# First expert layer's end summed by diagonal products, router indices reordered, and a written order for the causal attention's head groups

## The chip, the cores and the metric

The kernel runs on one NeuronCore of a Trainium2 chip. The metric is the time of one execution on the device in microseconds (us); the statement about the kernel before is the median of three runs. The program is written by hand for each engine: TensorE (PE; its weight loads are PEld), VectorE (DVE), ScalarE (ACT), GpSimd (POOL) and SyncE (SP), with semaphores between them. Each engine carries out its own list in order, so a wait holds up everything behind it on that engine.

## The reference, cut to what matters

There are 1,024 tokens of width 512. The six layers are: bottleneck layer, sigmoid attention, bottleneck layer, experts, causal attention, experts. Each begins with a layer norm.

```python
# experts (layers 4 and 6): H, F, E, K = 512, 800, 8, 2
logits = xt @ gate_w.T
top_vals, top_idx = top_k(softmax(logits), K)          # two of eight experts for each token
act = silu(x @ w1[e].T) * (x @ w3[e].T)
y   = sum over a token's two experts of weight * (act @ w2[e].T)
x   = x + 0.5 * y
# causal attention (layer 5): 32 heads of 16
q, k, v = x @ wq.T, x @ wk.T, x @ wv.T                 # q and k are rotated (rotary)
out = softmax(causal(q @ k.T / 4)) @ v
x   = x + out @ wo.T
```

## The kernel before, in words

The tokens lie in eight tiles of 128 rows (`X`, f32, in SBUF). A layer's front normalizes each tile on DVE (`bn_stats`, `bn_aggr`, then the subtraction and scaling), with POOL working out the reciprocal deviation between the last two; PE transposes the result and ACT copies it out of PSUM. `dve_front` (L463) interleaves the tiles: in turn n it does the update of tile n, the statistics of n-1, the normalization of n-2 (in layers 5 and 6) and the moments of n-1.

**Experts.** `dve_moe` sorts the 2,048 (token, expert) pairs into 72 blocks of 32 rows, which form four streams of 18 steps. The router is a chain of small DVE operations (L1131 to L1184): one-hot matrices OHL (L1160) and OHH (L1162 to L1165), a product of 16 small matmuls on PE that inverts the permutation (L1011), then the indices GIDX for the gather (L1178 to L1180). Between the two lie the experts of the blocks (EBC to EBX, L1168 to L1174) for which SP waits before it issues the step's weight loads (L921, L874), and FALL (L1175), for which ACT waits. PE fills its waits with throw-away bf16 products (`pe_awake`, L996): 14 while the router works and 18 while the first rows are gathered. A weight load whose expert has not changed, or was guessed right, is skipped by its condition.

A step is 128 rows: `up` (L1033), SiLU on ACT (L1093), product and block transposes on DVE (L1205, L1221), `down` (L1052) and the last 32 inner columns (L1066). ACT copies the result (L1105) and POOL scatters it to DRAM (L979). At the layer's end SP and ACT wait for the last scatter (`y_out`), and each issues eight loads of rows (`rows_back`, L960), SP those of a token's first expert and ACT those of its second. DVE adds the two, weighted, with two operations on each tile (L1226, L1227), in `dve_front`'s turn.

**Between experts and attention.** `sp_attn1_weights` (L1358) waits for the last product (`m_y`), then issues three loads of 1,024 KB: the q and k weights into WRAW and the v weights into WQKV. After its row loads, ACT reorders q and k in 16 copies (L1372). PE waits for the first updated tile, does ten throw-away products and then the fronts of tiles 0 to 3 with three such products between them (`pe_front_attn1`, L1446), and then projections (L1432).

**Causal attention.** Eight groups of four heads. All engines follow one list, `PLAN1`, made by `plan_attn1` (L1249). Its units in a group are: 32 `max` (PE scores for the row maxima, L1480; DVE takes the maximum, L1638), `shift` (DVE, L1643 to L1647) and `mtr` (PE transposes L1487, DVE copy L1655, SP sends the result, L1406); 48 `exp` (PE scores L1504, and the mask L1507 on a diagonal tile; ACT exponential L1585); 12 `av` (PE products with the values, L1517); 2 `oc` (ACT copy L1592) and 2 `turn` (PE transposes L1526; DVE L1663, L1664). The maxima run ahead of the exponentials: each unit of group g has a due time, from a count of the columns before it, with `LEAD1 = 1.25` groups taken off for the maxima, and the list is sorted by it. `max`, `mtr` and `turn` share four PSUM banks in a ring (`lay_ring`): a `max` of over 512 columns, an `mtr` and a `turn` take two neighbouring banks, other maxima one. PE waits before each of them until DVE has done with what was in the banks. The `exp` units have three banks, `av` one.

## Time and profile before

| | us |
|---|---|
| median of 3 runs (1286.12 to 1288.74) | 1287.13 |
| the profiled execution | 1285.68 |
| its span in the trace | 1283.8 |
| PE busy in the span | 1176.7 (92%) |
| DVE busy | 869.8 (68%) |
| ACT busy | 356.2 (28%) |
| POOL busy | 141.0 (11%) |

In the timelines each row is: start, duration, engine, line, operation, output<-input, count, and in brackets how long the engine sat idle before it and what ended that. The time from one row's start to the next is called its pitch below; it is shorter than the duration where operations overlap in the pipeline. The stages lie as follows in the span: first router about 183 to 201, first expert layer to 503, front and projections of attention to 635, head groups to 889, output product and second router to 953, second expert layer to the end.

### The profile page before, as it was taken

The page shows a single profiled execution, that of the slowest core. Times are in us where ns is not written, and L with a number is a line of the kernel's source. Part 1 is how long each engine was busy: PE and PEld are TensorE (multiplying, and loading weights), DVE is VectorE, ACT ScalarE, POOL GpSimd, SP SyncE. Part 2 cuts the span into 40 slices and gives each one's busy share as a digit, 9 for nine tenths or more (in the row PEclk, how much of TensorE's full clock was granted, in tenths as well). Part 3 has the DMA queues.
Part 4 walks back from the last instruction along what each step waited for, and adds up shares of the span by engine and source line. Part 5 has one row for each costly group of instructions (what it writes and reads, how often), then busy time and mean ns, then how long its engine had stood idle before and what let it go on. Part 6 is the DMA issues. An engine that isn't in the chain of part 4 may idle for free.

```text
span 1283.8 us, 28073 instructions
## 1 busy us (share of the span) xinstructions
PE 1176.7 (92%) x9925; PEld 507.6 (40%) x9925; DVE 869.8 (68%) x2481; ACT 356.2 (28%) x744; POOL 141.0 (11%) x191
## 2 busy tenths in 40 slices
PE   7799979999999995799999999998989899999992
PEld 3478553333333331343333333333644233333330
DVE  4832666877777762778888888850458677777763
ACT  5434611000000000322266666665200000000010
POOL 2200011111111100442000000000110101111000
PEclk9899969999999998899999999999979999999996
DMA  9100342258714354429514332003951645615556
GB/s 361 43 1 1 152 159 101 62 193 297 253 53 153 100 174 150 151 76 191 129 27 83 51 47 31 2 2 123 390 193 35 255 141 202 202 52 186 183 186 239
DMA packets 63667, 174.31 MB, mean 136 GB/s; under 512 B 9885, under 2 KB 16627, under 8 KB 61351
## 3 DMA queue, kind: packets, MB, share of 16 engines
q1 hardware_dynamic: 54319, 148.50, 35.9%
q0 software_dynamic: 5760, 18.88, 4.4%
q10 hardware_dynamic: 3448, 5.14, 1.2%
q8 instruction: 78, 1.28, 0.4%
q14 instruction: 62, 0.51, 0.1%
HBM read 785.47 MB, written 22.03 MB: 629 GB/s over the span
## 4 chain that ended last, share of the span: by engine, by line
PE 77%; DVE 11%; DMA 5%; ACT 3%; issue 3%; SPq 2%; POOL 0%; ACTq 0%; POOLq 0%; DVEq 0%
PE PS L1033 29%; PE PS L1052 13%; PE PS L1517 6%; PE PS L1480 5%; PE PS L1504 4%; PE PS L760 3%; PE PS L744 2%; PE PS L1544 2%; PE PS L1432 2%; PE PS L524 2%; DVE PS L1638 2%; PE PS L1066 1%; PE PS L508 1%; DVE STAT L472 1%; DMA split_scratch<-arena 1%
## 5 line engine op out<-in xcount | busy, mean ns | idle before, releaser
L1033 PE MATMUL PS<-arena 128*32 128x400 f32 x3456 | 394.4, 499 | 7.9 <-DMA HH<-in_w 3.9
L1033 PE MATMUL PS<-HH,arena 128*32 128x400 f32 x1152 | 393.8, 500 | 0.0
L1033 PEld LDWEIGHTS PS<-arena 128*32 128x32 f32 x3456 | 143.4, 110 | 252.4 <-issue 244.3
L1221 DVE STREAM_TRANSPOSE arena<-arena 32x192 f32<-32x192 f32 x576 | 211.3, 367 | 7.2
L1638 DVE CUSTOM_DVE_ANT_0 PS<-PS,U 128x128 f32<-128x128 f32 (+7 forms) x256 | 187.8, 785 | 35.4 <-PE PS L1480 34.4
L1052 PE MATMUL PS<-arena 128*32 128x512 f32 x1512 | 193.8, 596 | 4.0 <-DVE arena L1221 4.0
L1585 ACT ACTIVATE arena<-PS 128x512 f32<-128x512 f32 (+3 forms) x384 | 165.1, 497 | 74.5 <-PE PS L1507 49.0
L1199 DVE STREAM_TRANSPOSE arena<-arena 32x128 f32<-32x128 f32 x544 | 164.5, 302 | 17.9 <-DMA arena<-h_scratch,RT 9.9
L1093 ACT ACTIVATE arena<-PS 128x400 f32<-128x400 f32 x72 | 36.2, 503 | 432.3 <-PE PS L1033 432.3
L1205 DVE TENSOR_TENSOR arena<-arena,PS 128x400 f32<-128x400 f32 x72 | 41.0, 571 | 131.9 <-ACT arena L1093 131.9
L1033 PEld LDWEIGHTS PS<-HH,arena 128*32 128x32 f32 x1152 | 124.7, 110 | 0.0
L1504 PE MATMUL PS<-arena 99*128 99x512 bf16 (+3 forms) x384 | 111.2, 328 | 3.9 <-ACT arena L1585 2.2
L1480 PE MATMUL PS<-arena 96*128 96x512 bf16 (+3 forms) x384 | 101.0, 328 | 11.0 <-DVE arena L1638 6.2
L1052 PEld LDWEIGHTS PS<-arena 128*32 128x32 f32 x1512 | 56.2, 111 | 127.5 <-issue 121.7
L1052 PE MATMUL PS<-HH,arena 128*32 128x512 f32 x216 | 100.3, 601 | 0.0
L1517 PE MATMUL PS<-arena 128*32 128x512 f32 (+3 forms) x768 | 80.2, 497 | 0.0
L969 POOL DMA_INDIRECT arena<-h_scratch,RT x36 | 35.2, 978 | 356.1 <-DVE arena L1199 309.6
L490 POOL TENSOR_SCALAR VE<-MV 128x1 f32<-128x1 f32 (+1 forms) x44 | 12.8, 290 | 489.3 <-DVE MV L480 416.0
L1480 PEld LDWEIGHTS PS<-arena 96*128 96x128 bf16 x384 | 30.6, 97 | 80.0 <-DVE arena L1638 51.6
L979 POOL DMA_INDIRECT y_scratch<-arena,RT x36 | 35.5, 986 | 236.5 <-ACT arena L1105 231.6
L1432 PE MATMUL PS<-HH,arena 128*128 128x512 f32 x128 | 57.9, 613 | 1.6 <-ACT HH L532 0.9
L1504 PEld LDWEIGHTS PS<-arena 99*128 99x128 bf16 x384 | 36.9, 97 | 54.5 <-ACT arena L1585 35.0
(247 smaller groups left out, 1239.2 us busy)
## 6 DMA issues: line engine op xcount, KB each, us to landing
arena<-in_w SPq DMA_DIRECT2D x456, 800.0 KB
arena<-in_w2a SPq DMA_DIRECT2D x266, 768.0 KB
HH<-in_w SPq DMA_DIRECT2D x152, 800.0 KB
HH<-in_w2a SPq DMA_DIRECT2D x38, 768.0 KB
arena<-split_scratch SPq DMA_DIRECT2D x96, 128.0 KB, 6.8
split_scratch<-arena SPq DMA_DIRECT2D x8, 768.0 KB, 5.6
arena<-in_w2b SPq DMA_DIRECT2D x72, 64.0 KB
U<-in_w2b SPq DMA_DIRECT2D x72, 64.0 KB
```

The source lines that it names most:

```text
L760: mm = eng.matmul(PS[:, bank, jj * P:(jj + 1) * P], AT0[:, m % 4, j * P - a:(j + 1) * P - a], h_in[:, i, h * P:(h + 1) * P], start=(i == 0 ...
L1033: mm = eng.matmul(PS[SR * j:SR * j + SR, 2 * hf + m, 0:FH], XBT[:, u, c, SR * j:SR * j + SR], W13[j][:, c // 2, m, c % 2, hf * FH:(hf + 1) ...
L1052: mm = eng.matmul(PS[SR * j:SR * j + SR, 4 + u, :], ACT_T[:, u, c, SR * j:SR * j + SR], half_of(j, half)[:, c % (FC // 2), :], start=(c == ...
L1199: tr = eng.transpose(XBT[SR * b:SR * b + SR, u, :, SR * a:SR * a + SR], src[:, :, SR * b:SR * b + SR])
L1205: eng.tensor_tensor(half, half, PS[:, 2 * hf + 1, 0:FH], ALU.mult).then_inc(S("m_act"), 1)
L1221: tr = eng.transpose(ACT_T[SR * b:SR * b + SR, u, :, rows], src[:, :, SR * b:SR * b + SR])
L1432: mm = eng.matmul(PS[:, at + par, :], WQKV[:, x, c, first:first + P], HS[k][1][:, c, J * HT_:(J + 1) * HT_], start=(c == 0), stop=(c == C ...
L1480: mm = eng.matmul(PS[:, b + lo // HT_, 0:hi - lo], QT[0:KS, slot, h, i * P:(i + 1) * P], KT[0:KS, slot, h, lo:hi], start=True, stop=True)
L1504: mm = eng.matmul(bank[:, 0:hi - lo], KT[0:KS + 3, slot, h, i * P:(i + 1) * P], QT[0:KS + 3, slot, h, lo:hi], start=True, stop=not diag, s ...
L1517: mm = eng.matmul(PS[32 * h:32 * h + 32, 7, lo - J * HT_:HT_], VA[:, i, (GH * g + h) * VC:(GH * g + h) * VC + 32], PB[:, n % 3, h, 0:hi - lo],
L1585: eng.activation(PB[:, (n // GH) % 3, h, 0:hi - lo], PS[:, 4 + n % 3, 0:hi - lo], ACT.Exp, scale=SCALE1).then_inc(S("s_p"), 1)
L1638: eng.tensor_tensor_reduce(scores, scores, MASKW[:, T - wide:T], 1.0, HOLE, ALU.add, ALU.max, MP[:, g % 2, h, i:i + 1]).then_inc(S("s_md"), 1)
```

## The change

Four things change together.

**The first expert layer's end.** WRAW moves to where the weights of stream 1 lie. The k weights are loaded on SP as soon as the last `up` is done (before the last step's `down` weights); those of q and v follow behind the last step's loads, with no wait for `m_y`. SP issues all 16 row loads, tile by tile; ACT none, and it reorders the weights as soon as its last copy is done, k first. DVE makes eight matrices (`DIAG`, 128x128, identity times a column of weights) after its last transposes. For tiles 0 to 3 (`SUMMED`) PE adds the two weighted rows, as two f32 products with `DIAG` in a bank (`pe_sum_rows`), and DVE adds the bank to X in one operation. PE does 34 throw-away products after its last `down`, then the four sums, then the fronts with two such products between them. The DVE order of the front is written out in `dve_front_attn1`.

**The router.** The eight operations on constants (L1120 to L1127) move ahead of the last two `dve_top` of the first expert layer. OHH's third part is made ahead of OHL, its second part by ACT (`s_rowed`), and PE waits for both `s_low` and `s_rowed`. FOUND, FROM and GIDX come ahead of EBC to EBX and FALL.

**The front of the sixth layer.** The last tile's `bn_aggr` comes ahead of the normalization of tile 6.

**The attention's list.** The due times give way to a written order of 98 units for every group (`GROUP1`): m is the next of the maxima, `shift` and `mtr`, e an `exp`, a an `av`, c an `oc`, t a `turn`. A group's order begins with the last `av`, `oc` and `turn` of the group before as its first a, c, t. Ahead of it run the 34 units of group 0 and ten of group 1.

```diff
-        WRAW = arena[:, 26464:26464 + 2 * C * D].rearrange("p (n c d) -> p n c d", n=2, c=C)
+        at = 7584 + 2 * (2 * C * FF + FC * D)
+        WRAW = arena[:, at:at + 2 * C * D].rearrange("p (n c d) -> p n c d", n=2, c=C)
+        DIAG = arena[:, at + 2 * C * D:at + 2 * C * D + 8 * P].rearrange("p (n d) -> p n d", d=P)
+        SUMMED = (0, 1, 2, 3)
...
+        def dve_front_attn1(eng, k, update):
...
+            for n in range(4):
+                update(n)
+                if n >= 1:
+                    stats(n - 1)
+                if n >= 2:
+                    normal(n - 2)
+                if n >= 1:
+                    moments(n - 1)
+            stats(3)
+            normal(2)
+            moments(3)
+            for n in range(4, NT):
+                update(n)
+                if n == 4:
+                    normal(3)
+                stats(n)
+                if n > 4:
+                    normal(n - 1)
+                moments(n)
+            normal(NT - 1)
...
+                if p == NSTEP and f == 0:
+                    eng.wait_ge(S("m_h"), 2 * NSTEP)
+                    eng.dma_start(WRAW[:, 1], A["wqkv"][:, 1]).then_inc(S("s_wraw1"), 16)
...
             for i in range(NT):
                 rows_back(eng, i, 0)
+                if f == 0:
+                    rows_back(eng, i, 1)
...
             if f == 0:
                 eng.drain().then_inc(stage_end, 1)
+                pe_awake(eng, 0, 34)
+                eng.wait_ge(S("s_diag"), 1)
                 pe_front_attn1(eng, k + 1)
...
+        def pe_sum_rows(eng, k, i):
+            eng.wait_ge(yl_in[i], 16 * TOPK)
+            if i >= 2:
+                eng.wait_ge(s_x, NT * (k + 1) + i - 1)
+            for j in range(TOPK):
+                mm = eng.matmul(PS[:, 6 + i % 2, :], DIAG[:, TOPK * i + j, :], YT[:, i, j, :], start=(j == 0), stop=(j == TOPK - 1))
+            mm.then_inc(S("s_sum"), 1)
...
         def act_moe(eng, link, k, f):
+            eng.wait_ge(S("s_high"), f + 1)
+            eng.activation(OHH[:, :, 1, :], OHH[:, :, 2, :], ACT.Copy, scale=row_of[:]).then_inc(S("s_rowed"), 1)
...
+            if f == 0:
+                eng.wait_ge(S("m_h"), 2 * NSTEP)
+                for i in SUMMED:
+                    for j in range(TOPK):
+                        dg = eng.tensor_scalar(DIAG[:, TOPK * i + j, :], ident[:], WT[:, i, j:j + 1], None, ALU.mult)
+                dg.then_inc(S("s_diag"), 1)
+
             def add_rows(i):
+                if f == 0 and i in SUMMED:
+                    eng.wait_ge(S("s_sum"), i + 1)
+                    eng.tensor_tensor(X[:, i, :], X[:, i, :], PS[:, 6 + i % 2, :], ALU.add).then_inc(s_x, 1)
+                    return
...
-        LEAD1 = 1.25
+        GROUP1 = ("emememeacmeetemeaemememeaemeemeaemeemeacemeteemam"
+                  "meemmemeameemeemmaeeeeammmeeemmemamemeeeamememeea")
...
+                next_of = dict(zip("meact", (later, iter(exps), iter(sums), iter(copies), iter(turns))))
+                for kind in GROUP1:
+                    u = next(next_of[kind], None)
+                    if u is not None:
+                        plan.append(u)
...
         def sp_attn1_weights(eng):
-            eng.wait_ge(S("m_y"), NSTEP)
-            for n in (1, 0):
-                eng.dma_start(WRAW[:, n], A["wqkv"][:, n]).then_inc(S("s_wraw"), 16)
+            eng.dma_start(WRAW[:, 0], A["wqkv"][:, 0]).then_inc(S("s_wraw0"), 16)
             eng.dma_start(WQKV[:, 2], A["wqkv"][:, 2]).then_inc(S("s_wv"), 16)
...
         def pe_front_attn1(eng, k):
-            eng.wait_ge(s_x, NT * k + 1)
-            pe_awake(eng, 0, 10)
+            for i in SUMMED:
+                pe_sum_rows(eng, k - 1, i)
             for i in range(4):
                 pe_front(eng, k, i)
                 if i < 3:
-                    pe_awake(eng, 0, 3)
+                    pe_awake(eng, 0, 2)
```

## Rows read from the trace of the kernel before

**Rows 1.** The page, part 4: the chain that ended last, by engine.

```profile
PE 77%; DVE 11%; DMA 5%; ACT 3%; issue 3%; SPq 2%; POOL 0%; ACTq 0%; POOLq 0%; DVEq 0%
```

**Rows 2.** POOL, SP, DVE and PE timelines at the first expert layer's end.

```profile
503.28 0.97 POOL L979 DMA_INDIRECT y_scratch<-arena,RT  x1 [7.35 <-ACT arena L1105]
...
502.42 0.84 SPq L1362 DMA_DIRECT2D arena<-in_wqkv  x2
...
510.75 4.35 SPq L960 DMA_DIRECT2D arena<-y_scratch  x8
...
514.47 0.75 DVE L1226 SCALAR_TENSOR_TENSOR X<-arena,RT,X 128x512 f32<-128x512 f32 x1 [18.52 <-DMA arena<-y_scratch]
...
531.34 9.43 PE L1432 MATMUL PS<-HH,arena 128*128 128x512 f32 x16 [0.88 <-ACT HH L532]
```

**Rows 3.** Busy time by stretch: engines, PE clock, DMA share, GB/s, first layer's end.

```profile
506.00:508.00 2.00, 0.00 (x0) 0.00 (x0) 0.00 (x0) 0.00 (x0) 0.00 (x0) 0.50 1.00 385
```

**Rows 4.** POOL and DVE timelines at the second expert layer's end.

```profile
1261.40 0.97 POOL L979 DMA_INDIRECT y_scratch<-arena,RT  x1 [9.05 <-ACT arena L1105]
...
1267.70 0.75 DVE L1226 SCALAR_TENSOR_TENSOR X<-arena,RT,X 128x512 f32<-128x512 f32 x1 [15.33 <-DMA arena<-y_scratch]
```

**Rows 5.** Chain of waits (start, us, what) and DVE timeline: a projection, a PSUM addition.

```profile
541.64 6.87 PE PS L1432 x16
...
920.64 0.69 DVE L1669 TENSOR_TENSOR X<-X,PS 128x512 f32<-128x512 f32 x1 [2.99 <-PE PS L1544]
```

**Rows 6.** DVE, PE and SP timelines, first router; last row the second router's PE.

```profile
183.45 0.06 DVE L1120 MEMSET RT<- 128x4 uint32 x1 [0.24 <-DVEq L158]
...
184.69 0.29 DVE L1131 TENSOR_TENSOR RT<-small,RT 128x128 f32<-128x128 f32 x1
...
194.62 0.21 DVE L1178 COPY RT<-PS 128x54 f32<-128x54 f32 x1
...
193.49 0.57 PE L1011 MATMUL PS<-arena 128*128 128x54 bf16 x16 [1.85 <-DVE arena L1165]
193.91 5.73 PE L996 MATMUL PS<-identb 128*128 128x512 bf16 x18
199.79 0.66 PE L1017 MATMUL PS<-ident,arena 128*128 128x128 f32 x4
...
199.12 0.13 SPq L874 DMA_DIRECT2D HH<-in_w  x1
...
951.38 0.66 PE L1017 MATMUL PS<-ident,arena 128*128 128x128 f32 x4 [0.17 <-DMA arena<-h_scratch,RT]
```

**Rows 7.** DVE timeline: the same maximum, one head group apart.

```profile
647.38 0.97 DVE L1638 CUSTOM_DVE_ANT_0 PS<-PS,U 128x768 f32<-128x768 f32 x1
...
679.66 0.97 DVE L1638 CUSTOM_DVE_ANT_0 PS<-PS,U 128x768 f32<-128x768 f32 x1
```

**Rows 8.** PE timeline inside a head group.

```profile
655.94 1.07 PE L1517 MATMUL PS<-arena 128*32 128x512 f32 x8
656.94 0.39 PE L1504 MATMUL PS<-arena 99*128 99x512 bf16 x1
657.16 0.22 PE L1507 MATMUL PS<-mask_st,identb 128*128 128x128 bf16 x1
657.22 0.59 PE L1480 MATMUL PS<-arena 96*128 96x512 bf16 x2
657.66 0.38 PE L1504 MATMUL PS<-arena 99*128 99x512 bf16 x1
...
659.20 0.34 PE L1480 MATMUL PS<-arena 96*128 96x384 bf16 x1 [0.67 <-DVE arena L1638]
```

**Rows 9.** DVE timeline beside it; last two rows: groups of instructions (total, mean | idle), 640 to 840 us.

```profile
657.86 1.23 DVE L1638 CUSTOM_DVE_ANT_0 PS<-PS,U 128x1024 f32<-128x1024 f32 x1 [0.71 <-PE PS L1480]
...
L1638 DVE CUSTOM_DVE_ANT_0 PS<-PS,U 128x768 f32<-128x768 f32 (+1 forms) x199 | 146.0, 784 | 30.6 <-PE PS L1480 29.8
...
L1480 PE MATMUL PS<-arena 96*128 96x512 bf16 (+3 forms) x298 | 80.1, 328 | 7.4 <-DVE arena L1638 4.0 <-DVE HH L1664 2.5
```

120 lines of the change are left out of this document (65 added, 55 removed).

## The prediction

> **What bounds the kernel now.** I read the chain of waits first, then busy time by stretch, then the timelines of the three places that the change touches. TensorE carries 77% of the chain and VectorE 11% [rows 1]: most of the span is matmul that this change leaves alone. What can move is time in which PE stands waiting, and there are three such places.
>
> The first expert layer's end. POOL issues the last scatter at 503.28, the first updated tile starts on DVE at 514.47, and attention's first projection starts at 531.34 [rows 2]. That is 28 us with almost no matmul. Just before the scatter, at 502.42, SP has put 3 MB of attention weights in the queue, and the DMA engines are full (share 1.00, 385 GB/s) while every engine idles [rows 3]. The second expert layer has the same end without those loads: there the first tile starts 6.30 us after the scatter's issue (1261.40 to 1267.70), against 11.19 here [rows 4].
>
> The routers, where a chain of small DVE operations leads to the gather [rows 6].
>
> The head groups. The same maximum returns after 32.28 us, group after group [rows 7]. I add up what a group gives PE by pitches [rows 8]: 512 bf16 columns 0.22, a mask 0.06, an `av` of 512 columns 1.00. Maxima and exponentials have 18,432 columns each, so 36 x 0.22 = 7.9 twice; 32 masks 1.9; the twelve `av` make nine full ones, 9.0; the transposes of `turn` and `mtr` I estimate at 1.5, by their count and the mask's pitch, those of f32 at twice that. Sum 28.2, so some 4.1 us of a group is stall. On the other side DVE waits for maxima 29.8 us in 200, or 4.8 in a group [rows 9]. Neither engine is full; the order makes them wait for one another.
>
> **The change part by part.** The sum is made against the profiled execution, 1285.68 (span 1283.8 and 1.9 around it), which lies 1.45 below the median 1287.13; what I subtract from the one I subtract from the other.
>
> *Router.* Eight constant operations, 184.69 - 183.45 = 1.24 us, leave the first layer's chain [rows 6]. Their new place is ahead of two `dve_top`, where DVE waits for PE's logits; without that cover they would cost their 1.24 again. Moving one part of OHH to ACT takes some 0.2 off DVE (bounds 0 and 0.5, a small operation here being 0.2 to 0.3); ACT's copy, with its added wait, runs beside OHL, and only ACT's exponential is queued behind it. FOUND started at 194.62 although PE's product was over at 193.49 + 0.57 = 194.06 [rows 6]; in front of EBC it gains those 0.5. The indices come 0.7 earlier, but PE does not follow: its 18 throw-away products start behind the inversion and end at 193.91 + 5.73 = 199.64, and the gathered rows are taken at 199.79 [rows 6]. So the filler is what ends last next. First layer: 1.24 + 0.2 = 1.4 gained. Second layer: there PE waited 0.17 for the gather [rows 6], so 0.2 + 0.17 = 0.4.
>
> Against it, SP's release (`s_eb`) now stands behind GIDX, about 1.0 later in the chain. The fourth of step 0's first weight issues ended at 199.25 [rows 6], and `up` starts about 1.3 after 199.79, so the slack was 1.9. It shrinks to 1.9 - 1.0 - 0.2 = 0.7, in the second layer to a little less. These loads are skipped ones, and no row shows how long such a one takes to its semaphore: cost between 0 and 1.2 in each layer. I take 0.4 over both, nearer to 0 since no byte moves. Router in all: -1.4, between -2.7 and +0.6. The sixth layer's earlier `bn_aggr` costs or gives at most its 0.2; it counts as zero, since PE has logits to do there.
>
> *First layer's end.* The k weights go out some 13 us earlier and the others about 6, so that at the 385 GB/s of rows 3 the last 2 MB are through in 5.4 us, before the scatter. The wait added on SP ahead of the `down` loads is for an `up` that PE has already finished, so they are not held up; they are preceded by 1 MB, by the same rate 2.7 us of transfer, before a product that starts more than 5 us later. Then the first rows should be there 6.3 us after the scatter, as in rows 4. SP issues both rows of a tile itself: eight issues took 4.35 [rows 2], so one more takes 0.5. First rows at 503.28 + 6.3 + 0.5 = 510.1, against 514.47. Two diagonal products at full clock (16 of that size in 6.87, 0.43 each [rows 5]) take 0.9: sum at 511.0.
>
> From there DVE sets the pace. An addition from PSUM lasts 0.69 [rows 5] and takes 0.60 to the next; it replaces 2 x 0.75 overlapping to 1.43. Tiles 0 to 3 take four additions and four statistics (8 x 0.60), three normalizations (0.45) and four moments (0.10): 6.55. Once DVE waits 0.65 for the second tile: eight row loads of 256 KB in 4.35 us of issue are also about the memory's rate, some 1.25 a tile. That gives 518.2. The update of tile 4 by the old pair (1.4), the fourth normalization (0.5, and 0.3 for POOL), transposes and ACT copy (1.3) lead to the first projection at 521.7, against 531.34: -9.6. ACT's 16 copies no longer stand in the way, and the other row loads are covered, SP being 8.7 us over 16 issues while DVE takes 1.8 or more a tile. The first 16 projections took 9.2 us against 6.87 [rows 2, 5], the clock being low at first. I leave that as it is, since the fronts stay sparse; if the added work keeps it up, 2.3 more come. If the scatter is as slow as before, 4.9 are lost. DVE's eight diagonal matrices are hidden behind the last `down`; the 34 fillers start at 502.4 and take 0.22 each like the 512 columns of rows 8, 7.5 us, to 509.9, just ahead of the rows; at the lower clock they would take 15.0, to 517.4. The last `down` leaves the clock full, so I do not count that. Behind it all projections follow one another on PE, so the gain should stay. -9.6, between -4 and -12.
>
> On the scatter the rows show 4.9 us between an end with loads in the queues and one without [rows 2 to 4]. The Trainium skill ("DMA: Bandwidth & Descriptors", Queues, rings and completion order) says that each DMA engine takes turns between queues packet by packet. By that a scatter of 256 KB on POOL's queue would lose only about as much as its own transfer, some 0.7 us, and the sum would be -5.4 for this part. The measured difference speaks against it, as long as it is this contention that the two ends differ by.
>
> *Head groups.* Work is the same; only the order differs. The clearest stall before: DVE waits 0.71 for the widest maximum, which stands behind an `av` and an `exp`, and then PE waits 0.67 at the third maximum after it, whose bank that one holds [rows 8, 9]. I went through the ring for both orders: for each maximum, PE's work since the unit that holds its banks against DVE's time for that unit. Before, three units in a group come too early by this, by 1.0 together; in the written order none by more than 0.01. A walk through its dense stretch (the maxima of the last head and `shift`) finds no stall; through its last stretch, after `mtr`, two of 0.4 and 0.3, where maxima stand thick between short exponentials. PE's visible waits at maxima were 7.4 us in 6.2 groups, 1.2 each [rows 9]; the rest of the 4.1 is small steps and waits under modelled ends. I take 1.2 as the gain: 2.2 of ring waits by this, less 0.7 and some for what follows. Between the first exponentials and the last maxima there are 7.4 such groups: -8.9. Bounds: +3 for an order that stalls elsewhere, and 7.4 x 2.2 = -16; the whole 4.1 cannot go. The opening list is bound by DVE in both orders: zero, to 1 either way.
>
> Sum: -1.4 - 9.6 - 8.9 = -19.9. The profiled execution would be 1265.8, the median 1287.1 - 19.9 = 1267.2, so 1267.
>
> **The rivals.** *The order gives nothing.* PE and DVE trade one wait for another, since DVE needs 27.5 of the 32.3 us and any burst fills the ring again. For it: the largest stretch in which DVE's work exceeds PE's is as large in the new order (2.1 us) as in the old (2.0). Against it: the ring count above. Time: 1287.1 - 11.0 = 1276.
>
> *The scatter stays slow,* because what delays it is not the weight loads but its own place: the first layer's last rows, or writes to DRAM that wait for something else. For it: no row shows this scatter alone. Against it: rows 4. Then 4.9 less: 1272. The Trainium skill's taking turns between queues, above, would come out here at 4.2 less.
>
> *Slower.* The place is the list's second half, `aeeeeamm` and `meeemmem`: four `exp` in a row want three banks of ACT's, and the maxima behind `mtr` find the ring full, so that DVE first starves and then holds PE. A group would have to take 34.0 us instead of 32.3 to eat up the other two parts (11.0 / 7.4 = 1.5, and 0.35 for the bound of no change); at 2.5 more a group it gives 1287.1 - 11.0 + 18.5 = 1294.6. Against it: the total work per group, 28.2, would have to carry 7 us of stall.
>
> *The fillers or sums run at the lower clock.* The rows wait behind fillers until 517.4, 7.3 later than they land; DVE then no longer waits for tiles, which gives 0.65 back, so 6.7 of the 9.6 go: 1274. For it: PE's clock was at 0.50 by 506 [rows 3], but only after idling, which the fillers prevent.
>
> **How the numbers follow.** Forecast 0.60; order gives nothing 0.17; scatter slow 0.10; lower clock 0.08; slower 0.03; the remaining 0.02 is a change that cancels itself. A measurement of this kernel can tell about 0.2% (2.6 us) from no change. The range takes in the rivals at 1272, 1274 and 1276 with the router's bound above them, and below the forecast the full ring gain and clock, short of both bounds at once: 1255 to 1279. Faster 0.94, same 0.03, slower 0.03.
>
> **What would show it.** The first row update on DVE (now an addition from PSUM) within 8 us of the scatter, not 11; the first projection near 522; a group's period near 31.1 and the wait of 0.67 before the third maximum gone; the gather's transposes 1.4 and 0.4 sooner, with a wait on a weight load at step 0 if `s_eb` is too late. A period still at 32.3, or a first projection after 527, would make the prediction wrong.

## The result and the profile after

The changed kernel took 1277.33 us (median of 5 runs, 1274.53 to 1279.13) against 1287.13 (5 runs, 1286.12 to 1288.95): ratio 0.9922, 95% interval 0.99 to 0.9944. That is 9.8 us less, where 20.1 were forecast. Measured again, it took 1275.7, ratio 0.9908 (0.9882 to 0.9934). The profiled execution took 1278.5, its span is 1276.6.

First the chain of waits of the kernel after, by engine, beside [rows 1]:

```profile
PE 77%; DVE 10%; DMA 4%; ACT 3%; issue 3%; SPq 1%; POOL 1%; POOLq 0%; ACTq 0%; DVEq 0%
```

DVE, DMA and SP's queue gave up a point each. To see where the rest of the forecast went, I cut both spans at the same events and subtract (each number is the start of an instruction in the timelines, after minus before):

| stretch | before | after | difference | forecast |
|---|---|---|---|---|
| start to SP's first guessed load | 183.29 | 184.05 | +0.76 | 0 |
| to the first SiLU product on DVE | 28.05 | 29.64 | +1.59 | -1.2 |
| to the last scatter of layer 4 | 291.94 | 293.65 | +1.71 | 0 |
| to the third block of projections | 46.87 | 37.92 | -8.95 | -9.6 |
| to group 0's `mtr` copy | 80.39 | 79.91 | -0.48 | 0 |
| to group 1's `mtr` copy | 31.42 | 33.57 | +2.15 | 0 |
| to the output product | 228.71 | 220.95 | -7.76 | -8.9 |
| to the second layer's first SiLU product | 72.25 | 75.49 | +3.24 | -0.2 |
| to its last scatter | 298.48 | 299.51 | +1.03 | 0 |
| to the end | 22.40 | 21.91 | -0.49 | 0 |
| sum | 1283.8 | 1276.6 | -7.20 | -19.9 |

The two large parts came nearly as forecast. What is missing lies mostly in five stretches that were written off at zero or taken for gains.

Each column is one profile, and some rows are less firm than they look. The changed kernel's second profile agrees with its first within 0.35 us in every row down to the output product, but has 77.25 and 297.94 in the second layer's two rows. The first guessed load stands between 180.9 and 187.7 in the nineteen profiles of this document, so the +0.76 of the first row says nothing.

**First layer's end.** POOL, SP, PE and DVE timelines of the kernel after, answering to [rows 2]:

```profile
507.34 0.97 POOL L1041 DMA_INDIRECT y_scratch<-arena,RT  x1 [9.06 <-ACT arena L1181]
...
510.12 8.35 SPq L1022 DMA_DIRECT2D arena<-y_scratch  x16
...
506.55 7.51 PE L1058 MATMUL PS<-identb 128*128 128x512 bf16 x34
513.90 7.36 PE L1151 MATMUL PS<-arena 128*128 128x512 f32 x16
...
515.82 0.69 DVE L1299 TENSOR_TENSOR X<-X,PS 128x512 f32<-128x512 f32 x1 [15.81 <-PE PS L1151]
517.86 0.69 DVE L1299 TENSOR_TENSOR X<-X,PS 128x512 f32<-128x512 f32 x1 [1.35 <-PE PS L1151]
...
528.77 4.53 PE L1510 MATMUL PS<-HH,arena 128*128 128x512 f32 x10 [0.88 <-ACT HH L589]
```

From the scatter's issue to the first row load 2.78 us (before 7.47), to the first diagonal product 6.56, to the first projection 21.43 (before 28.06). The 16 diagonal instructions for eight products take 7.36: a product is two instructions of 0.43 and more, so a tile's sum takes 1.8 us, not 0.9. DVE waits 1.35 for the second tile.

**Routers.** PE timeline of the kernel after at the first router, then busy time by stretch there (columns as in [rows 3]), then PE at the second router; beside [rows 6]:

```profile
192.65 0.78 PE L1074 MATMUL PS<-arena 128*128 128x54 bf16 x16 [2.54 <-DVE arena L1230]
193.26 5.16 PE L1058 MATMUL PS<-identb 128*128 128x512 bf16 x18
200.45 0.66 PE L1080 MATMUL PS<-ident,arena 128*128 128x128 f32 x4 [2.03 <-DMA arena<-h_scratch,RT]
201.78 0.54 PE L1096 MATMUL PS<-arena 128*32 128x400 f32 x3 [0.67 <-ACT arena L1160]
```

```profile
196.00:198.00 2.00, 2.00 (x11) 0.88 (x9) 0.81 (x5) 0.00 (x0) 1.16 (x2) 1.00 1.01 422
198.00:200.00 2.00, 0.43 (x2) 0.00 (x0) 0.00 (x0) 0.00 (x0) 0.00 (x0) 1.00 0.65 212
...
202.00:204.00 2.00, 2.00 (x20) 0.66 (x16) 1.91 (x8) 1.03 (x1) 0.81 (x1) 0.59 0.27 47
```

```profile
942.18 0.66 PE L1080 MATMUL PS<-ident,arena 128*128 128x128 f32 x4 [3.32 <-DMA arena<-h_scratch,RT]
```

POOL's row for the gather, before and after:

```profile
196.12 1.22 POOL L969 DMA_INDIRECT arena<-h_scratch,RT  x1 [22.63 <-DVE RT L1180]
```

```profile
194.97 1.22 POOL L1031 DMA_INDIRECT arena<-h_scratch,RT  x1 [20.72 <-DVE RT L1236]
```

The indices are there earlier: the gather is issued 10.92 us behind the first guessed load, not 12.84, which is the 1.9 that the prediction had for them. But the gathered rows are not: PE now idles 2.03 and 3.32 us for them, where fillers or 0.17 stood before. The DMA engines run at share 1.01 and 422 GB/s until just before the rows arrive. And once PE has idled, its granted clock falls to 0.59 in 202 to 204, which is the lower of its two levels, 1.2 GHz, for most of it, so the first `up` takes about 1.7 more.

**Head groups.** DVE timeline, the same maximum one group apart; groups of instructions between 640 and 840 us (total, mean | idle); and PE at group 0's `mtr`. They stand beside [rows 7, 9]:

```profile
653.08 0.97 DVE L1716 CUSTOM_DVE_ANT_0 PS<-PS,U 128x768 f32<-128x768 f32 x1 [0.30 <-PE PS L1558]
...
683.86 0.97 DVE L1716 CUSTOM_DVE_ANT_0 PS<-PS,U 128x768 f32<-128x768 f32 x1 [0.30 <-PE PS L1558]
```

```profile
L1716 DVE CUSTOM_DVE_ANT_0 PS<-PS,U 128x896 f32<-128x896 f32 (+1 forms) x210 | 155.1, 786 | 16.4 <-PE PS L1558 15.8
...
L1558 PE MATMUL PS<-arena 96*128 96x512 bf16 (+3 forms) x314 | 81.2, 328 | 0.0
```

```profile
624.53 0.61 PE L1565 MATMUL PS<-identb,arena 128*12 128x128 bf16 x8 [2.63 <-DVE arena L1725]
```

A group takes 30.78 us, 1.50 less than 32.28. PE's wait at maxima is gone altogether (7.4 to 0.0), DVE's is halved (29.8 to 15.8). But in the opening list `mtr` now stands right behind the `shift` it depends on, and PE waits 2.63 there (1.14 before). The first exponential comes 9.49 us after the `mtr` copy, not 4.85.

### The profile page after: what moved, and what is told of

It is laid out like the page before. It is cut to its first block, busy times and chain, and to the rows that moved or that the text cites. A ratio compares the mean times of both kernels' runs of the same rounds, so it can differ in the third digit from the quotient of the medians.

```text
span 1276.6 us, 28155 instructions
## 1 busy us (share of the span) xinstructions
PE 1186.2 (93%) x9962; PEld 513.8 (40%) x9962; DVE 869.9 (68%) x2483; ACT 355.9 (28%) x746; POOL 139.2 (11%) x191
## 4 chain that ended last, share of the span: by engine, by line
PE 77%; DVE 10%; DMA 4%; ACT 3%; issue 3%; SPq 1%; POOL 1%; POOLq 0%; ACTq 0%; DVEq 0%
PE PS L1096 30%; PE PS L1115 13%; PE PS L1595 6%; PE PS L1582 5%; PE PS L1558 5%; PE PS L817 3%; PE PS L801 2%; PE PS L1622 2%; PE PS L1129 1%; PE PS L1515 1%; PE PS L581 1%; ACT arena L1663 1%; PE PS L565 1%; DVE PS L1716 1%; PE PS L1585 1%
## 5 line engine op out<-in xcount | busy, mean ns | idle before, releaser
L1096 PE MATMUL PS<-arena 128*32 128x400 f32 x3456 | 399.1, 504 | 7.6 <-DMA HH<-in_w 3.7
L1096 PE MATMUL PS<-HH,arena 128*32 128x400 f32 x1152 | 398.5, 504 | 0.0
```

The source lines that it names most:

```text
L1096: mm = eng.matmul(PS[SR * j:SR * j + SR, 2 * hf + m, 0:FH], XBT[:, u, c, SR * j:SR * j + SR], W13[j][:, c // 2, m, c % 2, hf * FH:(hf + 1) ...
```

## The experiments

Every kernel is the changed one with one edit, or with the edits named. Ratios are against the kernel before, run beside it. Those of the changed kernel are 0.9922 and 0.9908; 0.001 is 1.3 us. Each single profile carries clock dips of its own, so I read a part's effect from its own stretch first and from the ratio second. Where two intervals overlap, the times alone don't tell two kernels apart.

### Each part undone, and more fillers

**Router as before** (OHH by DVE alone, EBC to FALL before FOUND, constants back behind the logits).

> The changed kernel with the router part put back as before (constants, OHH, order of GIDX and EBC to EBX); the rest of the change stays. Theory A, the gather is bound by the guessed weight loads ahead of it in the DMA engines (it landed 16.4 us after SP's first of them in both kernels), so the earlier indices only empty PE, its clock falls and the first up product is 1.5 to 1.7 us longer in each expert layer: some 3 to 5 us faster than the changed kernel, 1273 to 1274, with both first up products at 10.95 us. Theory B, the low clock at the first up product is chance and the router part gains 1.4 + 0.4 as I forecast: some 2 us slower than the changed kernel, 1279.

Measured: 1272.9 us, ratio 0.9902 (0.9879 to 0.9925). First guessed load to first SiLU product 28.01, against 29.64 in the changed kernel and 28.05 before. PE timeline:

```profile
195.37 5.73 PE L1056 MATMUL PS<-identb 128*128 128x512 bf16 x18
201.21 0.66 PE L1077 MATMUL PS<-ident,arena 128*128 128x128 f32 x4
```

The fillers reach up to the transposes again. Those still come 16.46 us after SP's first guessed load (16.40 changed, 16.50 before): earlier indices did not move them by more than 0.1.

That is the first layer. In the second, undoing the router brings nothing back: the same way takes 29.35 us, against 29.38 in the changed kernel and 26.80 before, the rows are taken at 16.25 (16.38 and 15.26), and PE idles for them with the old router too:

```profile
935.97 0.66 PE L1077 MATMUL PS<-ident,arena 128*128 128x128 f32 x4 [2.85 <-DMA arena<-h_scratch,RT]
```

The interval of the ratio overlaps with both of the changed kernel.

**More fillers** behind the inversion.

```diff
-            pe_awake(eng, 1, 18)
+            pe_awake(eng, 1, 30)
```

> The changed kernel with 30 throw-away products in place of 18 behind the inversion, in both routers. Theory A: the gaps of 2.0 and 3.3 us ahead of the gathered rows are filled (12 x 0.22 = 2.6 us), the clock stays full and both first up products take 10.95 us instead of 12.65 and some 12.4: 2.5 to 3 us faster than the changed kernel, 1274.5. Theory B: the fillers end later than the gather or change nothing: 0 to 1 us slower, 1277 to 1278.

Measured: 1270.83 us, ratio 0.9883 (0.9856 to 0.991). PE timeline:

```profile
191.35 7.88 PE L1058 MATMUL PS<-identb 128*128 128x512 bf16 x30
199.06 0.60 PE L1080 MATMUL PS<-ident,arena 128*128 128x128 f32 x4
```

Transposes 16.93 behind the first guessed load, 0.5 later than in the changed kernel, and yet from there to the first SiLU product 11.49, not 13.24. So 1.7 of what the idle stretch costs is the clock behind it, and fillers save that. What the late rows themselves cost is seen further down, where the gather is freed.

**Old order of the head groups** (`plan_attn1` of before).

> The changed kernel with the attention's list by due times as before (LEAD1 = 1.25). The written order alone: a group 30.78 us instead of 32.28, some 10.5 us less over seven groups, but the opening, from mtr of group 0 to the first exponential, 9.5 us instead of 4.9. Theory A, both effects are the list's own: this kernel is 6 us slower than the changed one, 1283, its period 32.28 and its opening 4.9. Rival, the longer opening comes from the earlier projections (the split loads land late) and stays: 10 us slower, 1287.

Measured: 1282.09 us (12 runs), ratio 0.9968 (0.995 to 0.9987), 0.0046 to 0.006 above the changed kernel: the new order is worth 6 to 8 us. DVE timeline:

```profile
660.43 0.97 DVE L1717 CUSTOM_DVE_ANT_0 PS<-PS,U 128x768 f32<-128x768 f32 x1 [0.98 <-PE PS L1559]
...
692.72 0.97 DVE L1717 CUSTOM_DVE_ANT_0 PS<-PS,U 128x768 f32<-128x768 f32 x1 [0.98 <-PE PS L1559]
```

The period is 32.29 again, and group 0's `mtr` to group 1's takes 31.43 instead of 33.57, so the opening list's 2.1 us come from the new order too. Of these 1.7 are the clock: with PE idling 2.63 us at this place, it fell in six of the ten profiles that have this opening (33.57 in each), and in the other four, `a_old_router` and `a_fill30` among them, the stretch takes 31.9.

**Old end of the first layer** (loads, row loads, sums, fillers and the interleaved front all undone).

> The changed kernel with the first expert layer's end and attention's front as before. In the changed kernel the way from the last scatter to the third block of projections is 8.95 us shorter. Theory A, this gain is lasting: 8 to 9 us slower than the changed kernel, 1286; or 6.5 to 7.5 (1284.5) if the low clock in the last down product (1.6 us in the changed kernel's trace) comes from the part's weight load in front of it. Rival, the opening of the list takes most of it back: 3 to 4 us slower, 1281.

Measured: 1279.23 us, ratio 0.9933 (0.9907 to 0.9959), only 1.4 to 3.2 us above the changed kernel. In its profile the stretch from scatter to third projections is 44.46, 6.5 longer, but the second expert layer and its router happen to be 5.9 us shorter (last scatter 1255.14 against 1254.69). A later run takes the loads alone and finds their full price, so I don't take this small ratio for the part's worth; why it is so small stays open. Two things are to be read from the profile. The release is late again, at 7.44. And the first projections take 7.81 to the next block, as in the changed kernel and not 10.14 as before: that step doesn't need the new end.

### What holds up the gather; the other dips

**Guessed down loads behind the release.**

```diff
-            guess_in(eng, f, last)
+            for c in range(C):
+                up_in(eng, last, c, guess(last))
             eng.wait_ge(S("s_eb"), f + 1)
+            for half in range(2):
+                down_in(eng, last, half, guess(last))
```

> The guessed loads of the last stream's down weights (two of 768 KB) are issued behind the router's release, so behind the gather's issue, instead of ahead of it. Theory A (the gathered rows land only when the guessed weight loads ahead of them are through): 1.5 MB less at some 420 GB/s is 3.7 us, but the rest then comes against the gather's own issue, 196.7, so the transposes of the gathered rows come 1 to 3 us sooner: some 14.6 us behind SP's first guessed load instead of 16.4, in both routers; TensorE's idle time before them (2.0 and 3.3 us in the changed kernel) shrinks by as much, and its clock stays up in the first up. Time 2 to 7 us below the changed kernel, about 1273. Theory B (what ends last before the transposes is the index chain, or a fixed time of the indirect load): the transposes stay 16.4 behind the first guessed load and the time stays at 1277, within 1.5. If the down weights are then late, the first down product shows a wait on them.

Measured: 1277.94 us, ratio 0.9904 (0.9878 to 0.993). Windows (as above):

```profile
196.00:198.00 2.00, 0.92 (x5) 0.19 (x2) 0.45 (x3) 0.00 (x0) 0.96 (x1) 1.00 0.86 261
198.00:200.00 2.00, 0.00 (x0) 0.00 (x0) 0.00 (x0) 0.00 (x0) 0.00 (x0) 1.00 1.02 423
200.00:202.00 2.00, 1.04 (x4) 0.71 (x4) 0.00 (x0) 0.00 (x0) 0.00 (x0) 0.58 0.86 350
```

Neither outcome that I had written down. The transposes came 17.11 behind the first guessed load, at 200.96, later than before the edit. The 1.5 MB were issued at 194.99, 0.4 us behind the gather (194.57), and it was held up by them all the same. It did not wait for the last of them: the engines were still at share 0.86 when the rows were used, and 0.6 us earlier 0.25 MB of the down loads had yet to start. From 198 on packets of both queues move side by side.

**Fillers ahead of the last down product** (`pe_awake(eng, 7, 8)` before `down(NSTEP - 1)`).

> Eight throw-away products of 512 bf16 columns ahead of the last down product of each expert layer, where TensorE stands idle for about 2 us. Theory A (the 1.7 us more that one profile shows between the first product and the last scatter than another are the clock, which falls in that idle stretch in some executions): first product to last scatter takes 292 us in the profile, not 293.7, and the time is 0 to 3.4 us below the changed kernel, about 1275.5. Theory B (those 1.7 us have another cause, or the fillers only push the down product back): 293.7 stays, or the last scatter comes up to 1.8 us later, and the time is 1277 to 1281.

Measured: 1275.9 us, ratio 0.9891 (0.9865 to 0.9917). First product to last scatter 291.95, not 293.65: theory A. Over all profiles, the 2 us of idling at that place (1.97 in the kernel before too) cost 1.7 in nine of the twelve that have it, and not in the kernel before, `a_old_router` and `a_fill30`; none of the seven with fillers there loses it. But the row loads were released 4.35 behind the scatter here, not 2.78.

**`mtr` later in the opening list.**

```diff
+            front = [(at + 4.5 / ahead if u[0] == "mtr" else at, u) for at, u in front]
             plan += [u for _, u in sorted(front, key=lambda u: u[0])]
```

> In the opening list of the causal attention the transposes of group 0's maxima stand four units later, not right behind the shift that they wait for. Theory A (this place makes TensorE stand idle 2.6 us, and the clock that falls then costs 1.7 more at the first exponentials): that idle stretch is gone, first transposes to the second group's transposes takes about 31.5 instead of 33.6 us, and the time is 0.5 to 2.5 us below the changed kernel, about 1275.5. Theory B (the wait only moves to the first exponentials, which need what the transposes give): the first exponential keeps its time and the whole stays at 1277, within 1.

Measured: 1273.44 us, ratio 0.9871 (0.9842 to 0.9901), 0.0037 to 0.0051 below the changed kernel. No wait at `mtr` shows any more. From the third projections to group 1's `mtr` copy it takes 109.26, against 113.48 changed and 111.81 before: 4.2 gained. Some 2.2 of it are the wait and the rest is the clock, since the four profiles of the unedited opening in which the clock stays up have 111.35 to 111.59. So the forecast's "zero" held where the clock stayed up and was wrong by 1.7 where it fell, and a better place was worth 2.1 to 2.6.

**No diagonal sums** (`SUMMED = ()`; DVE adds both rows of every tile).

> Leaves the diagonal products out: the vector engine adds both rows of every tile itself, as before, but with the earlier loads, the fillers and the new interleaving of the front. Theory A (the sums are worth what they take off the vector engine's four first tiles, 0.8 us each, less the 1.75 us that a tile's two f32 products take): last scatter to first projection 23 to 24 us, against 21.4 in the changed kernel and 28.1 before; time 1.5 to 2.5 us above the changed kernel, about 1279. Theory B (the gain of this part is all in the sums, the earlier loads were hidden anyway): last scatter to first projection 26 to 28, time 1282 to 1284. Theory C (the sums gain nothing, as they take what they save): 21.4 and 1277.

Measured: 1276.0 us, ratio 0.9897 (0.9867 to 0.9926). Scatter to first projection 21.43, to the third block 37.93: the same to 0.01 us as with the sums. Theory C, by the stretch; the ratio can't tell it from the changed kernel's. DVE starts 1.64 earlier (6.84 after the scatter) and has 1.64 more to do. PE timeline:

```profile
519.48 1.12 PE L581 MATMUL PS<-ident,HH 128*128 128x128 f32 x4 [6.46 <-DVE HH L520]
```

PE idles 6.46 before it, and the transposes run at half clock; the last of them are at full clock again, just in time.

### Gather alone, loads alone, and two sums of edits

**Down loads held until the gathered rows are transposed** (and gone from `guess_in`, as above).

```diff
                 if p == 0:
+                    eng.wait_ge(S("s_xturn"), f + 1)
+                    for half in range(2):
+                        down_in(eng, last, half, guess(last))
```

> The guessed down loads (1.5 MB) go out only when TensorE has transposed the gathered rows, in both routers. The run before, with these loads right behind the release at 194.99, left a hole in the DMA engines at 195 to 197 and yet its gathered rows came no sooner. Theory A (the gathered rows land only when the DMA engines have nothing else left, whether it was issued before the gather or within a few us behind it): with the guessed up loads alone the engines are through at about 195, the gather lands by its own time, 3 to 4 us from its issue at 194.6, so the transposes come at 198 to 198.5, some 14 to 14.5 behind SP's first guessed load instead of 16.4; TensorE's idle time before them goes from 2.0 (3.3) to under 0.7 and the clock stays at 1.00 in the first up. That is 2 us in each router and up to 1.7 of clock in each: 3 to 7 us below the changed kernel. Theory B (the indirect load itself takes 5.5 us from issue to landing): transposes still 16.4 behind, no gain. Third outcome: the down weights are late for the first down product, which shows a wait on them; then the gain is less by that wait.

Measured: 1271.5 us, ratio 0.9893 (0.9861 to 0.9925). PE timeline:

```profile
193.27 4.04 PE L1063 MATMUL PS<-identb 128*128 128x512 bf16 x18
198.55 0.66 PE L1085 MATMUL PS<-ident,arena 128*128 128x128 f32 x4 [1.24 <-DMA arena<-h_scratch,RT]
200.09 0.54 PE L1101 MATMUL PS<-arena 128*32 128x400 f32 x3 [0.88 <-DMA HH<-in_w]
```

Transposes 14.30 behind the first guessed load (expected 14 to 14.5): theory A. The clock stays up; first guessed load to first product takes 26.04, 3.6 less than in the changed kernel. From its issue to the transposes the gather takes 3.58 with nothing in its way, and 5.48 in the changed kernel. In the kernel before it took 3.66: there the late indices and the gather's own time alone set 16.50, and the guessed loads, through at 13.96, held up nothing.

The wait of 0.88 at the first `up` is for SP's fourth skipped weight load: the product starts 0.11 us behind the end of that issue, so such a load takes next to nothing to its semaphore. SP's issues stand where they stood before (14.0 behind the first guessed load, 14.2 before); it is the rows that come early. In the second layer they stand 1.0 later than with the old router (14.3, not 13.3), the price that the prediction had for `s_eb`.

**Attention's weight loads late again,** all else as changed.

```diff
         def sp_attn1_weights(eng):
+            eng.wait_ge(S("m_y"), NSTEP)
+            eng.dma_start(WRAW[:, 1], A["wqkv"][:, 1]).then_inc(S("s_wraw1"), 16)
```

> The changed kernel, but with the three attention weight loads all issued behind the last product, as in the kernel before; sums, fillers and the new interleaving stay. Theory A (what delayed the last scatter before were these 3 MB in the queues): last scatter to the first sum on TensorE goes from 6.56 to 11 or 11.5 us, and scatter to first projection from 21.4 to 26; time 4 to 5 us above the changed kernel, and more where the low clock meets the sums. Theory B (the delay was in the place of the row loads, or in ACT's issues): 6.56 stays, and the time too. Theory C (each DMA engine takes turns between the queues packet by packet, so a scatter of 256 KB loses only its own share): scatter to first sum 7.3 to 7.6, time 1 us above.

Measured: 1282.63 us (12 runs), ratio 0.9972 (0.995 to 0.9993), 6 to 8 us above the changed kernel. SP and PE timelines (scatter issued at 510.95):

```profile
518.68 3.65 SPq L1019 DMA_DIRECT2D arena<-y_scratch  x8
...
522.35 9.28 PE L1148 MATMUL PS<-arena 128*128 128x512 f32 x16 [4.68 <-DMA arena<-y_scratch]
```

Scatter to row loads 7.73, to the first sum 11.40: 4.84 more than with the early loads; rows 2 to 4 had said 4.9. To the first projection it is 28.19, where the kernel before has 28.06. So with the loads late nothing is left of the 6.6 us that the changed kernel gains up to there; 1.9 of that goes on the sums, which start 4.7 us behind the fillers and run partly at the lower clock (9.28, not 7.36). The DMA queues (packets, MB, share of the 16 engines) in the 4.3 us from the scatter's issue, then in the next 2.9:

```profile
q1 hardware_dynamic: 185, 1.38, 95.5%
```

```profile
q1 hardware_dynamic: 134, 0.97, 79.6%
q0 software_dynamic: 80, 0.26, 22.2%
```

Queue 0 is the scatter's. Its first packet starts 4.43 us after the issue, where it starts at 1.54 with the loads out of the way, and then its 80 packets take 2.7 us beside the loads, where they take 0.8 alone. The release comes while the loads still run. The Trainium skill ("DMA: Bandwidth & Descriptors", Queues, rings and completion order) says that each engine takes turns between the queues packet by packet. The second step looks like that. By turns alone my estimate was 0.7 for the whole delay, and 2.9 of the 4.8 lie ahead of the first packet; what holds that one back no run shows.

**Two sums of edits.** `c_best_old`: router as before with 22 fillers, fillers ahead of the last down, `mtr` later. `c_best_new`: the changed router, down loads held back, and the same other two.

> Everything of the change but its router part, with 22 throw-away products behind the inversion instead of 18, 8 ahead of the last down product of each expert layer, and group 0's maxima transposes four units later in the opening list. If the effects seen alone add up: router undone 4.4, last down 1.7 to 3, opening list 3 to 6, below the changed kernel, so 8 to 12 us: ratio to the kernel before near 0.985, some 1268. If the clock's dips only move to another place: 3 to 5, ratio 0.989.

> The changed kernel with its own router, the guessed down loads held back until the gathered rows are transposed, the 8 throw-away products ahead of the last down product, and group 0's maxima transposes four units later. Theory A of the first run of this call: as good as the old router or 1 to 2 us per router better, ratio 0.981 to 0.985, some 1264 to 1268. Theory B (the indices' earlier arrival is worth nothing, whatever the queues hold): 4 to 5 us worse than the old router with 22 products, ratio 0.988.

Measured: 1270.91 us, ratio 0.9888 (0.9861 to 0.9915), and 1268.33, ratio 0.9864 (0.9837 to 0.9891). The first gave less than the sum of its parts (0.985); I take it that the effects seen alone were partly the same dips and partly chance, which no run separates. The second was 2.6 better, just short of what theory A said, but the two intervals overlap.

### Old or new router, and the late release

**Both raw weights early** (`d_early`: `c_best_new`, and WRAW[:, 0] issued with WRAW[:, 1]); **the same with the old router** (`d_early_old_router`); **the changed kernel again.**

> c_best_new (the guessed down loads behind the gathered rows, 8 throw-away products ahead of the last down, group 0's maxima transposes four units later), and the raw q weights go out with the raw k weights, 3 to 5 us before the last down loads instead of behind them. Theory A (the last scatter waits for whatever large loads still move; in c_best_new 1 MB of q and 1 MB of v were in the engines until 502, two us behind its issue): scatter to the first row load's issue goes from 4.95 back to 2.8, scatter to the first sum from 8.43 to 6.6, and first projection comes 1.5 to 2 us sooner behind the scatter (23.3 to 21.5). Time 1.5 to 2 us below c_best_new, ratio near 0.985. Theory B (the 1 MB more ahead of the last down loads makes that product late): a wait of 1 to 2 us on a weight load at the last down product, and nothing gained.

> d_early with the router as in the kernel before. Theory A (with the guessed loads out of the gather's way the indices are what ends last, so their 1.4 us count): transposes of the gathered rows 1 to 1.5 us later behind SP's first guessed load than in d_early (15.5 to 16 against 14.4), in the first layer; but the step's weight loads are released earlier, so the 0.9 us that TensorE waits for a weight load at the first up in c_best_new goes; net d_early better by 0.3 to 0.8 in the first layer and by 0 to 0.5 in the second, 1 us in all. Theory B (the reorder is a loss by itself): d_early_old_router 2 us or more faster.

> The changed kernel as it is. Its ratio to the kernel before was 0.992 with an interval of 0.99 to 0.9944. If medians of different calls can be compared by their ratios, it comes out in 0.990 to 0.994 again; if not, differences of 2 or 3 us between calls say nothing. In its profile I expect low clock in the first up of both layers again, since TensorE idles 2 to 3 us before them by construction, and at the last down product in about every other profile.

Measured: 1268.3 us, ratio 0.9852 (0.9825 to 0.988); 1266.53 us, ratio 0.9834 (0.9809 to 0.9859); 1275.7 us, ratio 0.9908.

Router: first guessed load to first product takes 26.05 with the new one, 27.97 with the old, so with the gather free the reorder gives 1.9 in the first layer, more than expected. In the second it takes 28.09 against 27.44. PE timeline of `d_early` there:

```profile
933.80 0.66 PE L1086 MATMUL PS<-ident,arena 128*128 128x128 f32 x4 [1.04 <-DMA arena<-h_scratch,RT]
935.87 0.54 PE L1102 MATMUL PS<-arena 128*32 128x400 f32 x3 [1.41 <-DMA HH<-in_w]
```

It waits twice, and the clock falls (it did not in the same place of `c_best_new` and `c_down_gathered`, at equal waits). So the reorder is no loss by itself and no clear gain in all; the two ratios can't be told apart.

Scatter: in `d_early` it was issued at 502.53, when the last large load had been through for 1.1 us, and yet the row loads came 4.71 behind it. Theory A fell. What all profiles with early loads and a late release share stands in the DMA queues in the 3 us from the scatter's issue, here of `d_early_old_router` (queue: packets, MB, share), with SP's timeline:

```profile
q0 software_dynamic: 76, 0.25, 21.7%
q8 instruction: 1, 0.02, 2.5%
```

```profile
507.15 6.88 SPq L1026 DMA_DIRECT2D arena<-y_scratch  x14
```

and of the changed kernel:

```profile
q0 software_dynamic: 80, 0.26, 22.8%
```

Queue 8 I read as TensorE's code: 79 packets in a span, and PE and PEld carry out 19,956 instructions, 253 a packet. Where such a packet falls into those 3 us, the release is late: 3.44 to 4.95 in six of the fourteen profiles with early loads up to here, against 2.77 to 2.79 in the other eight, and in all nineteen at the second layer's end, where none falls. In five of the six, three to five of the scatter's 80 packets are still missing after the 3 us. Full clock in the last down and a rest of the attention loads behind the scatter are not what does it: `a_old_router` has both (queue 1 busy until 1.20) and its release is at 2.78.

**The code moved.** Both are `d_early_old_router`: `e_pad30` with 30 products of 32 columns behind the 14 fillers, `e_fill4` with 4 fillers ahead of the last down, not 8.

> d_early_old_router with 30 tiny throw-away products (32 columns) behind the 14 at the router, where TensorE idles 1.9 us: they cost nearly nothing but shift all code behind by 60 instructions (matmul and weight load each). Theory A (the last scatter is signalled late because a load of TensorE's code falls just behind it): the load comes earlier, inside the last down product; no code load in the 3 us behind the scatter, and the row loads are released at 2.8 us instead of 4.2. First sum 1.4 sooner behind the scatter. Theory B (the release is late wherever the last down runs at full clock, for another cause): 4.2 to 5 again. Time: A, 0 to 1.4 below d_early_old_router; B, the same or up to 1 above, by the products.

> d_early_old_router with 4 instead of 8 throw-away products ahead of the last down product: code behind shifted by 8 instructions instead of 16. Theory A: the code load falls 8 instructions later, some 1 us, or still 2 to 3 us behind the scatter's issue where its bytes are already moved; release at 2.8 or up to 4. Theory B: release 4.2 to 5 as long as the clock is full. And whether 4 of them, 0.9 us of an idle stretch of 2 us, keep the clock up: first product to last scatter 292.0 if so, 293.7 if not.

Measured: 1267.71 us, ratio 0.9842 (0.9814 to 0.9869); 1268.97 us, ratio 0.9849 (0.982 to 0.9878). In `e_pad30` the code packet falls within 1 us of the scatter and the release is at 3.18. In `e_fill4` none falls into the 3 us. Its queues there, and SP's timeline (scatter at 507.54):

```profile
q0 software_dynamic: 80, 0.26, 22.9%
```

```profile
510.32 3.67 SPq L1026 DMA_DIRECT2D arena<-y_scratch  x8
```

The release is at 2.78, at full clock in the last down (first product to scatter 292.0), so theory B is out. In time it doesn't show: up to 1.4 us are below what the medians tell. By the time of its start the packet costs 0.4 (0.49 behind the issue), 0.7 (0.93), 1.3 to 1.6 (1.51 to 1.69) and 1.9 to 2.2 (2.07 and 2.23); the one at 3.39, in `b_no_sums`, costs nothing. Four fillers kept the clock as well as eight did.

The best kernel is `d_early_old_router`, 1266.53 us, with 1275.7 for the changed one and 1286.94 for the one before, run beside it; the intervals of the two ratios don't overlap. It has the head groups' order, the sums and both raw weights early, the guessed down loads behind the gather, fillers ahead of the last down, `mtr` later, and the old router. The change in the sixth layer's front was not run by itself.

## Why the prediction was half right

The direction and the range (1255 to 1279) held, and the two large parts came near their sizes, one of them partly by luck; the sum was twice too large.

**Router: the step that failed.** The prediction put it as "the filler is what ends last next", and took 1.4 off. What ends last once the indices are early is the gather, held up by the guessed weights that move beside it: its rows are taken at 16.40 behind the first guessed load, and at 14.30 with the guessed down loads out of its way. The rows of before hid this. There the indices came so late that the guessed loads were through (13.96) before the gather's own 3.66 us were over, and the fillers ended within 0.2 us of its rows. I read the fillers' end at 199.64 as if the rows had been there long before, and that no row said. In the first layer the true figure is +1.6 in the profile, all of it the clock. In the second it is +2.6 behind the first guessed load, again clock and rows that come 1.1 us later (16.38, not 15.26), but that this is the router's doing is not shown: with the router undone it is the same. The stall on skipped loads behind `s_eb` (0 to 1.2 forecast) exists, at 0.88 and 1.41, but shows only once the rows come early.

**Clock: the step left out.** I counted idle stretches opened by the change at nothing, and priced the low clock only at the end's fillers. Where the clock falls it costs some 1.7 us at each place where PE resumes a dense product. At the first `up`, behind waits of 2.0 to 4.0 us for the gathered rows, it fell in all sixteen cases; at the `mtr`, behind 2.63 us, in six profiles of ten; at the last down, behind 1.98 us, in nine of twelve. Adding PE's busy time times (1 - granted clock) over windows of 2 us gives 29.8 us in the profile before and 32.2 after, so 2.4 of the missing 12.7. Part of this is chance and not the change: the last down dips in the changed kernel, not in the one before, with the same wait in both.

**First layer's end: the wait right, the size partly luck.** Forecast -9.6, came -9.0. The contention was right (4.84 measured with the loads alone; 4.9 forecast), and the fillers ended just as the rows came, as forecast. But the first projection was 21.4 behind the scatter, not 18.4, so this step gave 6.6: 4.84 for the contention, and 1.8 for SP's row loads, fillers and interleaving together, which no run separates. The term "two diagonal products take 0.9" is 1.8, since a 512-column f32 product is two instructions, which the row "16 of that size in 6.87" already showed, being eight products. At 1.8 a tile, PE's sums and not DVE set the pace over the first tiles, and the sums give nothing. The other 2.3 are the clock in the first 16 projections (7.8 to the next block, 10.1 before), which I had named as possible and not counted. The profile with the old end has 7.8 too, and eight of the seventeen with the new end have 9.5 or more, so it is no effect of the part: it was luck that it filled the gap.

**Head groups: right.** Forecast 1.2 a group between bounds of -0.4 and 2.2; came 1.50, but only in the five full periods between the groups' `mtr` (the first and the last were 31.42 before), where I had counted 7.4. The two errors nearly cancel: 7.8 in all, 8.9 forecast. The ring count told which waits would go, and they went. The **opening list** at "zero, to 1 either way" held only where the clock stayed up. DVE bounds the list until a unit is placed where PE must wait for the end of DVE's chain, and the clock can fall in that wait; I had looked at the steady groups' order unit by unit and not at this one.

**Rivals.** "The order gives nothing" and "slower" fell with the period of 30.78; "the scatter stays slow" fell with a release at 2.78, the same as in the second layer; "fillers or sums at the lower clock" fell with a granted clock of 1.00 from 503 to 525.

## What to carry over

When a wait ends within a few tenths of a filler, the trace doesn't show what would end next; look for the resource that was busy until then (here the DMA engines at share 1.0) and ask what it would take to free it. Price each idle stretch that a change opens on PE not by its length alone but by the low clock behind it, and set fillers there. In a written order, look first at each unit that waits for another engine's chain, and put work between. And compare several profiles before explaining a stretch that differs by less than 3 us: the second router's +2.6 and the first projections' -2.3 both read like effects of the change, and both turn up without it.

## What was not expected of the hardware

A gather or scatter of 256 KB on POOL's queue is held up by SP's weight loads far beyond its own share of the bytes, even by loads issued 0.4 us behind it: the gather's rows were used 4.2 to 6.4 us after its issue instead of 3.6, and the scatter's first packet started after 4.4 us instead of 1.5. It does not wait until they have drained. A single 16 KB packet of what I read as TensorE's code, fetched within 2.3 us behind a scatter's issue, went with a completion 0.4 to 2.2 us later, so throw-away products put in 300 us earlier can move the end of a layer. That the packet is the cause rests on sixteen profiles and on moving it twice; by what way it delays the scatter no run shows. And equal idle stretches of 1.97 and 1.98 us ahead of the same product let the clock fall in one execution and not in another.
